# Expert results added into the output tensor, and router products with the weights stationary

## The chip, the cores and the metric

The kernel runs on one core of a Trainium2 chip. The metric is the time of one execution on the device in microseconds (us), as the median of several runs; the profile is of one more execution.

## The reference

A graph layer with 6250 nodes of 256 features (f32) and 100000 edges, followed by a mixture of experts. In short:

```python
xn = layernorm(x)
x = x + gnn(xn, W, edges) + linear_attention(xn, wq, wk, wv, wo)
z = layernorm(x)                       # 6250 x 256
logits = z @ Wr + br                   # 8 experts
top_p, top_idx = top_k(softmax(logits), 2)
weights = top_p / top_p.sum(-1)
zn = layernorm(z)                      # then one gain and bias for each expert
y_e = gelu((zn * g_e + b_e) @ W1_e + b1_e) @ W2_e + b2_e     # 256 -> 1024 -> 256
x = x + sum over the 2 picks of weights * y_pick
```

## The kernel before

The kernel is one program with an instruction stream written out by hand for each engine; semaphores order them. Tokens are cut into 49 tiles of 128 (the last has 106), and each stage streams over tiles. The stages in time:

- To about 490 us: edge lists are sorted, tokens normalized and projected. To about 1555 us: 832 chunks of gathered rows are summed by destination group (line 1437) and added into `acc` in SBUF, with the attention output beside them.
- **Router stage**, 1555 to about 1626 us. DVE computes statistics in four groups of tiles. ACT writes each normalized tile into `xs2` (two tiles make a pair, four pair buffers). For each pair TensorE transposes the four 128x128 blocks (`transpose_x2`, line 1470), ACT copies them from PSUM to `x2T` (`transposed_x2`; all ACT calls are recorded under line 1127), and TensorE multiplies (`router_product`, line 1477): for each token tile the 128x128 block of transposed tokens is the stationary operand and the 8 weight columns stream; the two halves of the features accumulate into 8 columns of bank `B[4]`. SP sends each pair of `xs2` to `token_x` in HBM (line 399) and then issues the load of all second-layer weights, 8 MB, into `W2A` (line 401). ACT scales `acc` afterwards.
- **Slot stage**, to about 1700 us. DVE picks the two best experts of each token, ranks the picks within each expert (with two matmuls), and deals them to 105 tiles of 128 slots, each tile of one expert. The experts of the tiles go by way of HBM (`slot_experts`, lines 406 and 408) to `expert_row`; DVE waits for the first of those transfers before `slot_digits`. 98 matmuls (line 1499) put the token and the pick of each slot into slot order. Slots are in token order within an expert. Unused slots get token 0, a pick whose gate is zero, and a row of their own behind the tokens of `sums` (`dump_row`). `sums` is an HBM tensor that SP sets from `acc` (line 426): the layer's result without the experts.
- **Expert stage**, to about 2467 us: for each slot tile t, POOL gathers the tokens (`gather_x`, line 513) and the gates (line 517); TensorE transposes the tokens (line 1518), multiplies with the first weights (line 1530), and, after ACT's gelu, with the second (line 1539); DVE adds the bias, multiplies with the gate and writes `y_out`, two buffers; POOL scatters it with an add in the DMA into `sums` (`scatter_y`, line 524). Each scatter waits for the one before to land, since two of them may hit one row. TensorE's order is: `inputs(0)`, `first_product(0)`, `inputs(1)`, then steps; step t is `first_product(t + 1)`, `inputs(t + 2)`, `second_product(t)`. DVE's is `inputs(0)`, `inputs(1)`, then steps of `inputs(t + 2)` and `outputs(t)`. SP loads the first weights of each tile, 1 MB (line 418), four buffers.
- **End**: SP waits for the last scatters and copies `sums` to the output, HBM to HBM (line 435).

DVE chains dependent small operations with a semaphore: `ch.add` issues one, `ch.sync` waits for all so far, `ch.link` does both.

Of the kernel before, what the change touches and what calls it, by code (L numbers as in the profile page):

```python
# [15 lines left out]
ALU = mybir.AluOpType  # L16
ACT = mybir.ActivationFunctionType
AX = mybir.AxisListType

P = 128  # L20
N_NODES = 6250
# [107 lines left out]
def gps_layer(nc, x, src, dst, src_rest, dst_rest, gnn_w, wq, bq, wkv, bkv, wo, bo,  # L129
              wr, br, ln_gT, ln_bT, w1, b1, w2, b2, out):  # L130
    ctx = ExitStack()
    with ctx:
# [6 lines left out]
        def dram(name, shape, dt):  # L139
            return nc.dram_tensor(name, shape, dt, kind="Internal").ap()  # L140
# [6 lines left out]

        sums = dram("sums", [(NT + 1) * P, D], F32)
        gates = dram("gates", [(PICKS + 1) * P, 1], F32)
# [17 lines left out]
        def grid(area, at, a, b, dt=F32):  # L167
            return piece(area, at, a * b, dt).rearrange("p (a b) -> p a b", b=b)
# [87 lines left out]
        wr_s, br_s = grid(BIG, 5448, KD, E), piece(BIG, 5464, E)  # L256
        stats2 = grid(BIG, 5150, NT, 6)
        expert_m8 = grid(BIG, 4192, NT, E)
        exp_tot, exp_tiles, exp_base, slot_e, exp_i = (piece(BIG, 4592 + 16 * k, E) for k in range(5))
# [7 lines left out]
        slot_at, slot_tile, pick_col = (piece(BIG, 5100 + 50 * k, PICKS, BF16) for k in range(3))  # L267
        row_1, dump_row, dump_pick = piece(BIG, 5250, 1), piece(BIG, 5251, 1), piece(BIG, 5252, 1)
        zero_row = BIG[0:1, 5260:5260 + ST].bitcast(BF16)
        row_f, tok_f, unused, unused_at, pick_f = (piece(BIG, 1600 + 110 * k, ST) for k in range(5))  # L270
        gates_T = BIG[0:NT, 5376:5376 + TOPK * P]
        slot_token, slot_row, slot_pick = piece(SMALL, 700, ST, I32), piece(SMALL, 0, ST, I32), piece(SMALL, 490, ST, I32)
        slot_eI = piece(BIG, 4690, 1, I32)
# [45 lines left out]
        router_in, norm2_ready = sem("router_in"), sem("norm2_ready")  # L319
        x2T_ps, x2T_ready, logit_ps = sem("x2T_ps"), sem("x2T_ready"), sem("logit_ps")  # L320
        res_ready, pc_rows = sem("res_ready"), sem("pc_rows")
        pick_ready, gap_ready, gap_exp, ranks_ps, places_ready = (
# [8 lines left out]
        y_ps, y_free, y_ready, y_sent = sem("y_ps"), sem("y_free"), sem("y_ready"), [sem("y_sent0"), sem("y_sent1")]  # L331
        o_sent = sem("o_sent")
        block = ctx.enter_context(nc.Block())
# [3 lines left out]
        def _(sp):  # L337
# [87 lines left out]
            sp.wait_ge(res_ready, 1)  # L425
            sp.dma_start(sums.rearrange("(t p) d -> p t d", p=P), acc).then_inc(sums_set, 16)
            with sp.Fori(1, ST // 4) as i:
                for s in range(4):
# [4 lines left out]
            sp.wait_ge(y_sent[1], 16 * (ST // 2))  # L433

            sp.dma_start(out.rearrange("(p a) d -> p (a d)", p=125), sums[0:N_NODES, :].rearrange("(p a) d -> p (a d)", p=125)
                         ).then_inc(o_sent, 16)
            sp.wait_ge(o_sent, 16)


        @block.gpsimd  # L440
        def _(pool):
# [78 lines left out]
            def scatter_y(t):  # L520
                pool.wait_ge(y_ready, t + 1)
                if t >= 1:
                    pool.wait_ge(y_sent[(t - 1) % 2], 16 * ((t + 1) // 2))
                pool.indirect_dma_start(sums, bass.IndirectOffsetOnAxis(ap=slot_row[:, t:t + 1], axis=0),  # L524
                                        y_out[t % 2], None, compute_op=ALU.add).then_inc(y_sent[t % 2], 16)

            pool.wait_ge(slots_ready, 1)
            for t in range(4):
                gather_x(t)
            pool.wait_ge(rows_known, 1)  # L530
            pool.wait_ge(gates_out, 32)
            for t in range(3):
                gather_gate(t)
            gather_x(4)
            pool.wait_ge(sums_set, 16)
            for t in range(ST):
# [8 lines left out]
        def _(dve):  # L545
# [479 lines left out]
            ch.add(ts(row_1, pcol, 1.0, ALU.add))  # L1025
            ch.add(ts(dump_row, pcol, float(NT * P + 1), ALU.add))
            ch.add(ts(dump_pick, pcol, float(PICKS * P + 1), ALU.add))
# [41 lines left out]
            dve.sem_inc(slots_ready, 1)  # L1069
            ch.add(dve.scalar_tensor_tensor(out=tok_f, in0=unused, scalar=dump_row, in1=tok_f, op0=ALU.mult, op1=ALU.add))  # L1070
            ch.add(dve.scalar_tensor_tensor(out=pick_f, in0=unused, scalar=dump_pick, in1=pick_f, op0=ALU.mult, op1=ALU.add))
            ch.sync()
            ch.add(dve.tensor_copy(slot_row, tok_f))
            ch.add(dve.tensor_copy(slot_pick, pick_f))
            ch.sync()
            dve.sem_inc(rows_known, 1)
            dve.wait_ge(gates_T_ps, 1)
# [33 lines left out]
            inputs(0, 0)  # L1111
            inputs(1, 1)
            for t in range(4):
                step(t, t)
# [8 lines left out]
        def _(act):  # L1123
# [118 lines left out]
            def transposed_x2(j):  # L1242

                n = min(2, NT - 2 * j)
                act.wait_ge(x2T_ps, j + 1)
                if j >= 4:
                    act.wait_ge(logit_ps, 2 * (j - 4) + 2)
                cp(x2T[j % 4][:, 0:n * KD, :], B[j % 4][:, 0:n * D].rearrange("p (g n) -> p g n", n=P)).then_inc(x2T_ready, 1)

            def roots(k):  # L1250
# [6 lines left out]
            for k, g in enumerate(LGROUPS):  # L1257
                act.wait_ge(norm2_ready, k + 1)
                for t in g:
                    j = t // 2  # L1260
                    if t % 2 == 0 and j >= 4:
                        act.wait_ge(x2T_ps, j - 3)
                        act.wait_ge(xs_out[j % 4], 16 * (j // 4))
                    cp(xs2[j % 4][:, t % 2, :], acc[:, t, :], ACT.Identity, scale=rstd2[:, t:t + 1], bias=nmr2[:, t:t + 1]
                       ).then_inc(xs_ready, 1)
                    if t % 2 == 1 and t >= 3:
                        transposed_x2(t // 2 - 1)
                    if t == g.stop - 3 and k + 1 < len(LGROUPS):
                        roots(k + 1)
            transposed_x2(NPAIR - 2)  # L1270
            transposed_x2(NPAIR - 1)
            for t in range(NT):
                last = cp(acc[:, t, :], acc[:, t, :], scale=dinv[:, t:t + 1])
# [31 lines left out]
        def _(pe):  # L1305
# [166 lines left out]

            def router_product(j):
                pe.wait_ge(x2T_ready, j + 1)
                for t in range(2 * j, min(2 * j + 2, NT)):
                    for k in range(KD):
                        last = mm(B[4][:, t * E:(t + 1) * E], x2T[j % 4][:, t % 2 * KD + k, :], wr_s[:, k, :],  # L1477
                                  start=k == 0, stop=k == KD - 1)
                    last.then_inc(logit_ps, 1)

            transpose_x2(0)
            for j in range(NPAIR):
                if j + 1 < NPAIR:
                    transpose_x2(j + 1)
                router_product(j)

            pe.wait_ge(pick_ready, 1)
# [65 lines left out]
            first_product(0, 0)  # L1553
            inputs(1, 1)
            step(0, 0)
            with pe.Fori(0, ST // 4 - 1) as i:
# [32 lines left out]
```

## Time and profile before

| | us |
|---|---|
| median of 3 runs | 2496.47 |
| lowest and highest | 2495.27, 2497.32 |
| profiled execution | 2495.66 |
| its span | 2493.8 |
| busy in the span: TensorE matmuls | 2173.1 (87%) |
| busy: POOL, DVE, ACT | 1381.6, 1156.7, 1143.8 |
| mean granted clock of TensorE | 0.93 |

The span runs from the first to the last recorded instruction; 1.9 us of the execution lie around it. The granted clock is a share of 2.4 GHz. The page has a chain of the work that ended last (half of it TensorE), groups of instructions by line with their busy time, mean duration and the idle time before them, and DMA issues with the time to their landing. The timeline gives instructions in order of time, neighbours of one kind merged (x32 is 32 of them), with the idle time in front of them and what ended it in brackets. An f32 product of TensorE shows as two records, a transpose as one.

### The profile page before, as it was taken

How to read it: one execution, taken by the hardware profiler on the slowest of the kernel's cores; microseconds unless marked ns; L12 is line 12 of the kernel's file. 1: busy time of each engine (PE TensorE's matmuls, PEld its weight loads, DVE VectorE, ACT ScalarE, POOL GpSimd, SP SyncE). 2: the span in 40 equal slices, each digit the busy share in tenths (PEclk: the TensorE clock that was granted, in tenths of full speed). 3: DMA queues.
4: the chain of work that ended last, by engine and by line, in shares of the span. 5: the costliest groups of instructions: out<-in, count | busy, mean ns of one | idle time of the engine just before them, and what ended most of it. 6: DMA issues, size and time to landing. Idle time of an engine off the chain costs nothing.

```text
span 2493.8 us, 50478 instructions
## 1 busy us (share of the span) xinstructions
PE 2173.1 (87%) x11949; PEld 1764.4 (71%) x11950; DVE 1156.7 (46%) x2139; ACT 1143.8 (46%) x2788; POOL 1381.6 (55%) x1357
## 2 busy tenths in 40 slices
PE   2996896588889999899899996858999999999995
PEld 1764774376766666666666665827999999999995
DVE  8885652155665665666665665362222222222221
ACT  3664114366666666666666664642223233232331
POOL 3420787277777777777777774003445454454542
PEclk9998667799999999999999999558999999999998
DMA  4002000333333333333333337366666665666664
GB/s 145 1 10 41 3 4 3 121 105 105 104 105 105 105 105 105 105 105 105 105 105 105 105 105 86 102 204 229 176 188 174 184 185 174 188 176 182 185 173 139
DMA packets 136541, 296.30 MB, mean 119 GB/s; under 512 B 28594, under 2 KB 78084, under 8 KB 136231
## 3 DMA queue, kind: packets, MB, share of 16 engines
q0 software_dynamic: 67552, 137.24, 21.7%
q1 hardware_dynamic: 68935, 158.44, 19.7%
q8 instruction: 22, 0.36, 0.1%
q14 instruction: 32, 0.26, 0.0%
HBM read 257.91 MB, written 40.92 MB: 120 GB/s over the span
## 4 chain that ended last, share of the span: by engine, by line
PE 50%; POOL 14%; issue 11%; DVE 10%; DVEq 10%; DMA 3%; SPq 1%; ACT 0%; POOLq 0%; ACTq 0%
PE B L1530 15%; PE B L1539 14%; PE B L1437 13%; POOL BIG L504 8%; POOL edge_rows L493 6%; DVE ACC L549 4%; DVEq L880 3%; DVEq L709 2%; DVEq L872 2%; PE B L1499 1%; PE B L1477 1%; DVE W2A L549 1%; PE B L1410 1%; DVE BIG L549 1%; DMA BIG<-table,W2A 1%
## 5 line engine op out<-in xcount | busy, mean ns | idle before, releaser
L504 POOL DMA_INDIRECT BIG<-table,W2A x832 | 786.6, 945 | 298.3 <-issue 224.2
L549 DVE TENSOR_TENSOR ACC<-ACC,B 128x512 f32 x832 | 572.2, 688 | 402.8 <-PE B L1437 295.8
L1127 ACT ACTIVATE BIG<-B,SMALL 128x128 f32<-128x128 f32 (+1 forms) x889 | 251.1, 387 | 523.9 <-PE B L1530 523.9
L1437 PE MATMUL B<-BIG,W2A 128*128 128x256 f32 x1664 | 411.2, 390 | 76.7 <-DVE ACC L549 49.2
L1437 PE MATMUL B<-BIG 128*128 128x256 f32 x1664 | 407.7, 389 | 45.3 <-DMA BIG<-table,W2A 24.1
L1437 PEld LDWEIGHTS B<-BIG,W2A 128*128 128x128 f32 x1664 | 286.4, 189 | 177.7 <-issue 150.4
L1437 PEld LDWEIGHTS B<-BIG 128*128 128x128 f32 x1664 | 294.6, 190 | 150.2 <-issue 110.6
L1530 PEld LDWEIGHTS B<-BIG,W1A 128*128 128x128 f32 x3360 | 393.7, 193 | 7.9 <-DVE BIG L552 2.6
L1530 PE MATMUL B<-BIG,W1A 128*128 128x128 f32 x3360 | 394.5, 276 | 2.0 <-DVE BIG L552 2.0
L1539 PE MATMUL B<-W2A,BIG 128*128 x1680 | 380.2, 379 | 0.8 <-DVE BIG L549 0.7
L524 POOL DMA_INDIRECT sums<-BIG,SMALL x105 | 170.6, 1625 | 335.9 <-DMA sums<-BIG,SMALL 279.2
L1539 PEld LDWEIGHTS B<-W2A,BIG 128*128 128x128 f32 x1680 | 311.0, 190 | 39.4 <-issue 1.4
L1127 ACT ACTIVATE W2A<-W2A 128x256 f32<-128x256 f32 x416 | 177.3, 496 | 199.2 <-PE B L1437 199.2
L1127 ACT ACTIVATE BIG<-W2A 128x256 f32<-128x256 f32 x416 | 177.4, 497 | 173.1 <-PE B L1437 173.1
L493 POOL DMA_INDIRECT edge_rows<-BIG x128 | 158.1, 1235 | 152.3 <-DVEq L765 111.0
L552 DVE TENSOR_SCALAR BIG<-B,SMALL 128x128 f32<-128x128 f32 x210 | 76.6, 407 | 291.4 <-PE B L1518 291.4
L1127 ACT ACTIVATE BIG<-B 128x256 f32<-128x256 f32 (+1 forms) x172 | 65.7, 411 | 292.4 <-PE B L1329 254.2
L549 DVE TENSOR_TENSOR BIG<-B,W1A 128x256 f32<-128x256 f32 x105 | 44.6, 425 | 272.2 <-PE B L1539 272.2
L513 POOL DMA_INDIRECT BIG<-token_x,SMALL x53 | 50.7, 956 | 177.0 <-DVEq L1069 161.1
L1127 ACT ACTIVATE BIG<-BIG,CONST 128x1024 f32<-128x1024 f32 x104 | 119.6, 1150 | 7.7
L1127 ACT ACTIVATE W2A<-W2A,CONST 128x1024 f32<-128x1024 f32 x104 | 119.4, 1148 | 7.7
L517 POOL DMA_INDIRECT BIG<-gates,SMALL x105 | 102.7, 978 | 32.0 <-issue 32.0
(234 smaller groups left out, 2086.8 us busy)
## 6 DMA issues: line engine op xcount, KB each, us to landing
W1A<-in_w SPq DMA_DIRECT2D x105, 1024.0 KB, 5.1
BIG<-table,W2A POOLq DMA_INDIRECT x832
W2A<-in_w SPq DMA_DIRECT2D x1, 8192.0 KB, 26.3
sums<-ACC SPq DMA_DIRECT2D x1, 6400.0 KB, 23.5
out_dram<-sums SPq DMA_DIRECT2D x1, 6250.0 KB, 21.7
token_x<-BIG SPq DMA_DIRECT2D x24, 256.0 KB, 2.1
W2A<-in_x SPq DMA_DIRECT2D x1, 3584.0 KB, 12.8
table<-ACC SPq DMA_DIRECT2D x2, 1792.0 KB, 10.6
```

The source lines that it names most:

```text
L493: pool.indirect_dma_start(edge_rows, bass.IndirectOffsetOnAxis(ap=row_all[:, r:r + 1], axis=0), keysI[0][:, ROW * r:ROW * (r + 1)], None). ...
L504: pool.indirect_dma_start(G[h][:, u, :], None, table, bass.IndirectOffsetOnAxis(ap=dst_T[:, c:c + 1], axis=0)).then_inc(gath[h][u // 2], 16)
L513: pool.indirect_dma_start(x_in[t % 4], None, token_x, bass.IndirectOffsetOnAxis(ap=slot_token[:, t:t + 1], axis=0)).then_inc(xs_in[t % 4], 16)
L517: pool.indirect_dma_start(slot_gate[:, t:t + 1], None, gates, bass.IndirectOffsetOnAxis(ap=slot_pick[:, t:t + 1], axis=0)).then_inc(gate_i ...
L524: pool.indirect_dma_start(sums, bass.IndirectOffsetOnAxis(ap=slot_row[:, t:t + 1], axis=0), y_out[t % 2], None, compute_op=ALU.add).then_i ...
L549: return dve.tensor_tensor(o, a, b, op)
L552: return dve.tensor_scalar(o, a, s1, s2, op0, op1)
L880: dve.drain()
L1127: return nc.scalar.activation(o, i, fn, **kw)
L1437: last = mm(B[u][:, k * D:(k + 1) * D], OH[h % 2][:, u, k * P:(k + 1) * P], G[h][:, u, :], start=True, stop=True)
L1530: last = mm(B[2 * s + c // 4][:, c % 4 * P:(c % 4 + 1) * P], w1_buf[s4][:, k, c * P:(c + 1) * P], x_inT[s][:, k, :], start=k == 0, stop=k ...
L1539: last = mm(B[7][:, 0:D], hidT[s][:, k, :], W2A[:, bass.ds(e * (KH * D) + k * D, D)], start=k == 0, stop=k == KH - 1)
```

## The change

The experts' results are scattered and added into the output tensor itself. `sums`, the final copy and the wait for it are gone; SP sets the output from `acc` in two transfers (48 full tiles, 106 rows). The output has no rows behind the tokens, so unused slots, which still add zero, must add it to token rows that no used slot of the same tile has. For each expert's last tile the kernel finds them: `offset_of` is each used slot's row less its position, `reached` compares it with every position, eight small matmuls count over the partitions, and the count plus the position is the row (`spare_f`). That is a chain on DVE in two halves with the matmuls between them, placed behind `inputs(1, 1)` on DVE and on TensorE. The picks of the slots have a semaphore of their own, `picks_known`; `rows_known` is signalled behind the new chain, and POOL waits for it ahead of the first scatter.

In the router the 8 weight columns are the stationary operand and 256 tokens stream, so logits come out with experts on 8 partitions, in `B[5]` and `B[6]` by turns; ACT copies them to `logits_T` (`transposed_logits`, one pair behind `transposed_x2`), and TensorE transposes them back to tokens (`token_logits`), one tile in one instruction.

```diff
@@ -255,6 +254,7 @@
+        logits_T = [W1A[0:E, R0 + 8 * NE + D * k:R0 + 8 * NE + D * (k + 1)] for k in range(2)]
...
@@ -423,7 +429,8 @@
             sp.wait_ge(res_ready, 1)
-            sp.dma_start(sums.rearrange("(t p) d -> p t d", p=P), acc).then_inc(sums_set, 16)
+            sp.dma_start(out[0:(NT - 1) * P, :].rearrange("(t p) d -> p t d", p=P), acc[:, 0:NT - 1, :]).then_inc(sums_set, 16)
+            sp.dma_start(out[(NT - 1) * P:N_NODES, :], acc[0:LAST, NT - 1, :]).then_inc(sums_set, 16)
...
@@ -431,10 +438,6 @@
             sp.wait_ge(y_sent[0], 16 * (ST // 2 + 1))
             sp.wait_ge(y_sent[1], 16 * (ST // 2))
-
-            sp.dma_start(out.rearrange("(p a) d -> p (a d)", p=125), sums[0:N_NODES, :].rearrange("(p a) d -> p (a d)", p=125)
-                         ).then_inc(o_sent, 16)
-            sp.wait_ge(o_sent, 16)
@@ -521,18 +524,19 @@
-                pool.indirect_dma_start(sums, bass.IndirectOffsetOnAxis(ap=slot_row[:, t:t + 1], axis=0),
+                pool.indirect_dma_start(out, bass.IndirectOffsetOnAxis(ap=slot_row[:, t:t + 1], axis=0),
                                         y_out[t % 2], None, compute_op=ALU.add).then_inc(y_sent[t % 2], 16)
...
-            pool.wait_ge(rows_known, 1)
+            pool.wait_ge(picks_known, 1)
             pool.wait_ge(gates_out, 32)
             for t in range(3):
                 gather_gate(t)
             gather_x(4)
-            pool.wait_ge(sums_set, 16)
+            pool.wait_ge(rows_known, 1)
+            pool.wait_ge(sums_set, 32)
@@ -1067,13 +1070,10 @@
             dve.sem_inc(slots_ready, 1)
-            ch.add(dve.scalar_tensor_tensor(out=tok_f, in0=unused, scalar=dump_row, in1=tok_f, op0=ALU.mult, op1=ALU.add))
             ch.add(dve.scalar_tensor_tensor(out=pick_f, in0=unused, scalar=dump_pick, in1=pick_f, op0=ALU.mult, op1=ALU.add))
             ch.sync()
-            ch.add(dve.tensor_copy(slot_row, tok_f))
-            ch.add(dve.tensor_copy(slot_pick, pick_f))
-            ch.sync()
-            dve.sem_inc(rows_known, 1)
+            ch.link(dve.tensor_copy(slot_pick, pick_f))
+            dve.sem_inc(picks_known, 1)
@@ -1110,6 +1110,36 @@
             inputs(0, 0)
             inputs(1, 1)
+
+            ch.add(dve.scalar_tensor_tensor(out=offset_f, in0=unused, scalar=float(NT * P), in1=row_f, op0=ALU.mult, op1=ALU.add))
+            ch.add(ts(slots_1, iota[:, 0:ST], 1.0, ALU.add))
+            ch.add(ts(last_end, exp_tiles, 0.0, ALU.is_gt))
+            ch.add(dve.memset(ones_2, 1.0))
+            ch.sync()
+            ch.add(ts(offset_f, offset_f, pcol, ALU.subtract))
+            ch.add(tt(last_end, last_end, exp_i, ALU.mult))
+            ch.sync()
+            for e in range(E):
+                ch.add(dve.scalar_tensor_tensor(out=last_of[:, e, :], in0=slots_1, scalar=last_end[:, e:e + 1], in1=offset_f,
+                                                op0=ALU.is_equal, op1=ALU.mult))
+            ch.sync()
+            ch.link(dve.tensor_reduce(offset_of, last_of, axis=AX.X, op=ALU.add))
+            for e in range(E):
+                ch.add(ts(reached[:, e, :], iota, offset_of[:, e:e + 1], ALU.is_ge))
+            ch.sync()
+            dve.sem_inc(spare_ready, 1)
+            dve.wait_ge(spare_ps, 1)
+            ch.link(dve.tensor_copy(before_of, B[5][:, 0:2 * E:2]))
+            for e in range(E):
+                ch.add(ts(last_of[:, e, :], slots_1, last_end[:, e:e + 1], ALU.is_equal, before_of[:, e:e + 1], ALU.mult))
+            ch.sync()
+            ch.link(dve.tensor_reduce(spare_f, last_of.rearrange("p e t -> p t e"), axis=AX.X, op=ALU.add))
+            ch.link(ts(spare_f, spare_f, pcol, ALU.add))
+            ch.link(tt(spare_f, spare_f, unused, ALU.mult))
+            ch.link(tt(spare_f, spare_f, row_f, ALU.add))
+            ch.link(dve.tensor_copy(slot_row, spare_f))
+            dve.sem_inc(rows_known, 1)
+
             for t in range(4):
                 step(t, t)
@@ -1244,8 +1274,16 @@
                 if j >= 4:
-                    act.wait_ge(logit_ps, 2 * (j - 4) + 2)
+                    act.wait_ge(logitT_ps, j - 3)
                 cp(x2T[j % 4][:, 0:n * KD, :], B[j % 4][:, 0:n * D].rearrange("p (g n) -> p g n", n=P)).then_inc(x2T_ready, 1)
+
+            def transposed_logits(j):
+
+                n = min(2, NT - 2 * j)
+                act.wait_ge(logitT_ps, j + 1)
+                if j >= 2:
+                    act.wait_ge(logit_ps, 2 * (j - 2) + 2)
+                cp(logits_T[j % 2][:, 0:n * P], B[5 + j % 2][0:E, 0:n * P]).then_inc(logitT_ready, 1)
@@ -1265,10 +1303,15 @@
                     if t % 2 == 1 and t >= 3:
                         transposed_x2(t // 2 - 1)
+                        if t >= 5:
+                            transposed_logits(t // 2 - 2)
...
             transposed_x2(NPAIR - 2)
+            transposed_logits(NPAIR - 3)
             transposed_x2(NPAIR - 1)
+            transposed_logits(NPAIR - 2)
+            transposed_logits(NPAIR - 1)
@@ -1471,18 +1514,29 @@
             def router_product(j):
+                n = min(2, NT - 2 * j)
                 pe.wait_ge(x2T_ready, j + 1)
+                if j >= 2:
+                    pe.wait_ge(logitT_ready, j - 1)
+                for k in range(KD):
+                    last = mm(B[5 + j % 2][0:E, 0:n * P], wr_s[:, k, :], x2T[j % 4][:, k:n * KD:KD, :],
+                              start=k == 0, stop=k == KD - 1)
+                last.then_inc(logitT_ps, 1)
+
+            def token_logits(j):
+                pe.wait_ge(logitT_ready, j + 1)
                 for t in range(2 * j, min(2 * j + 2, NT)):
-                    for k in range(KD):
-                        last = mm(B[4][:, t * E:(t + 1) * E], x2T[j % 4][:, t % 2 * KD + k, :], wr_s[:, k, :],
-                                  start=k == 0, stop=k == KD - 1)
-                    last.then_inc(logit_ps, 1)
+                    nc.tensor.transpose(B[4][:, t * E:(t + 1) * E], logits_T[j % 2][:, t % 2 * P:(t % 2 + 1) * P], ident[0:E, 0:E]
+                                        ).then_inc(logit_ps, 1)
...
                 router_product(j)
+                if j > 0:
+                    token_logits(j - 1)
+            token_logits(NPAIR - 1)
@@ -1552,6 +1606,10 @@
             first_product(0, 0)
             inputs(1, 1)
+            pe.wait_ge(spare_ready, 1)
+            for e in range(E):
+                last = mm(B[5][:, 2 * e:2 * e + 2], reached[:, e, :], ones_2, start=True, stop=True)
+            last.then_inc(spare_ps, 1)
             step(0, 0)
```

## Rows read from the trace of the kernel before

**Rows 1.** The page's costliest groups: TensorE in the expert stage.
```profile
L1530 PE MATMUL B<-BIG,W1A 128*128 128x128 f32 x3360 | 394.5, 276 | 2.0 <-DVE BIG L552 2.0
L1539 PE MATMUL B<-W2A,BIG 128*128 x1680 | 380.2, 379 | 0.8 <-DVE BIG L549 0.7
```

**Rows 2.** Timeline (start us, us, what), the end of the span.
```profile
2471.64 0.58 SPq L435 DMA_DIRECT2D out_dram<-sums  x1
```

**Rows 3.** Windows: stretch, its us, busy of each engine, PEclk, DMA, GB/s.
```profile
1548.00:1552.00 4.00, 2.06 (x9) 1.46 (x9) 1.87 (x4) 0.00 (x0) 0.00 (x0) 1.00 0.66 58
...
1556.00:1560.00 4.00, 0.00 (x0) 0.00 (x0) 3.50 (x16) 0.21 (x1) 0.00 (x0) 0.84 0.00 0
...
1608.00:1612.00 4.00, 4.00 (x21) 4.00 (x22) 0.00 (x0) 2.24 (x6) 0.00 (x0) 0.50 0.19 66
...
1644.00:1648.00 4.00, 0.00 (x0) 0.00 (x0) 3.64 (x11) 1.29 (x2) 0.00 (x0) 0.50 0.66 201
...
1704.00:1708.00 4.00, 3.10 (x21) 2.86 (x20) 0.71 (x2) 0.99 (x1) 1.60 (x2) 0.81 1.06 371
```

**Rows 4.** Timeline of the router stage.
```profile
1570.45 1.09 ACT L1127 ACTIVATE BIG<-ACC,SMALL 128x256 f32<-128x256 f32 x2 [3.22 <-DVEq L946]
...
1608.41 1.09 PE L1470 MATMUL B<-CONST,BIG 128*128 128x128 f32 x4
...
1609.30 1.72 PE L1477 MATMUL B<-BIG 128*128 128x8 f32 x8
...
1609.55 0.60 ACT L1127 ACTIVATE BIG<-B 128x512 f32<-128x512 f32 x1 [0.88 <-PE B L1470]
...
1610.04 1.08 ACT L1127 ACTIVATE BIG<-ACC,SMALL 128x256 f32<-128x256 f32 x2
...
1619.85 0.59 ACT L1127 ACTIVATE BIG<-ACC,SMALL 128x256 f32<-128x256 f32 x1
...
1623.84 0.38 ACT L1127 ACTIVATE BIG<-B 128x256 f32<-128x256 f32 x1 [1.43 <-PE B L1470]
...
1626.26 0.57 DVE L549 TENSOR_TENSOR W1A<-B,SMALL 128x392 f32<-128x392 f32 x1 [25.84 <-PE B L1477]
```

**Rows 5.** Timeline where the expert stage begins.
```profile
1700.82 6.06 PE L1530 MATMUL B<-BIG,W1A 128*128 128x128 f32 x32 [1.01 <-DVE BIG L552]
...
1707.29 0.73 DVE L552 TENSOR_SCALAR BIG<-B,SMALL 128x128 f32<-128x128 f32 x2 [6.52 <-PE B L1518]
...
1708.07 3.84 PE L1530 MATMUL B<-BIG,W1A 128*128 128x128 f32 x32 [0.97 <-DVE BIG L552]
...
1721.19 1.64 POOL L524 DMA_INDIRECT sums<-BIG,SMALL  x1 [15.28 <-DMA sums<-ACC]
```

**Rows 6.** Timeline around the transfer of the slot numbers.
```profile
1643.96 0.33 SPq L406 DMA_DIRECT2D slot_experts<-BIG  x1
...
1651.76 0.21 DVE L1036 CAST BIG<-BIG 128x98 bf16<-128x98 int32 x1
...
1652.04 0.25 SPq L408 DMA_DIRECT2D CONST<-slot_experts  x1
```

**Rows 7.** Timeline: DVE and TensorE operations like the added ones.
```profile
1645.90 0.56 DVE L1015 TENSOR_REDUCE SMALL<-W1A 128x49 f32<-128x392 f32 x1
...
1649.98 0.10 PEld L1494 LDWEIGHTS B<-BIG 1*128 1x128 bf16 x1 [12.83 <-DVEq L1030]
...
1694.09 0.46 DVE L552 TENSOR_SCALAR BIG<-BIG 128x105 f32<-128x105 f32 x3
...
1695.52 0.33 DVE L1070 SCALAR_TENSOR_TENSOR BIG<-BIG 128x105 f32<-128x105 f32 x1 [0.16 <-DVE SMALL L1068]
```

**Rows 8.** The tile `sums`: its scatters and what released them.
```profile
L524 POOL DMA_INDIRECT sums<-BIG,SMALL x105: 1570/1627/1650, 1721.2 to 2467.9; - x105
...
  DMA sums<-BIG,SMALL: 279.2, 92
...
DMA to landing us min/median/max: 3.7/6.5/23.5
```

More of the change, by code:

```diff
@@ L146, in gps_layer @@
         token_x = dram("token_x", [NT * P, D], F32)
-        sums = dram("sums", [(NT + 1) * P, D], F32)
         gates = dram("gates", [(PICKS + 1) * P, 1], F32)
@@ L267, in gps_layer @@
         slot_at, slot_tile, pick_col = (piece(BIG, 5100 + 50 * k, PICKS, BF16) for k in range(3))
-        row_1, dump_row, dump_pick = piece(BIG, 5250, 1), piece(BIG, 5251, 1), piece(BIG, 5252, 1)
+        row_1, dump_pick = piece(BIG, 5250, 1), piece(BIG, 5252, 1)
         zero_row = BIG[0:1, 5260:5260 + ST].bitcast(BF16)
@@ L271, in gps_layer @@
         gates_T = BIG[0:NT, 5376:5376 + TOPK * P]
+        last_of, last_end = grid(W1A, R0, E, ST), piece(W1A, R0 + 840, E)
+        spare_f, slots_1, offset_f = (piece(W1A, R0 + 850 + 110 * k, ST) for k in range(3))
+        offset_of, before_of = piece(W1A, R0 + 1180, E), piece(W1A, R0 + 1190, E)
+        reached = grid(W1A, R0 + 1200, E, P, BF16)
+        ones_2 = piece(W1A, R0 + 1720, 2, BF16)
         slot_token, slot_row, slot_pick = piece(SMALL, 700, ST, I32), piece(SMALL, 0, ST, I32), piece(SMALL, 490, ST, I32)
@@ L320, in gps_layer @@
         x2T_ps, x2T_ready, logit_ps = sem("x2T_ps"), sem("x2T_ready"), sem("logit_ps")
+        logitT_ps, logitT_ready = sem("logitT_ps"), sem("logitT_ready")
         res_ready, pc_rows = sem("res_ready"), sem("pc_rows")
@@ L331, in gps_layer @@
         y_ps, y_free, y_ready, y_sent = sem("y_ps"), sem("y_free"), sem("y_ready"), [sem("y_sent0"), sem("y_sent1")]
-        o_sent = sem("o_sent")
+        spare_ready, spare_ps, picks_known = sem("spare_ready"), sem("spare_ps"), sem("picks_known")
         block = ctx.enter_context(nc.Block())
@@ L1025, in _ @@
             ch.add(ts(row_1, pcol, 1.0, ALU.add))
-            ch.add(ts(dump_row, pcol, float(NT * P + 1), ALU.add))
             ch.add(ts(dump_pick, pcol, float(PICKS * P + 1), ALU.add))
```

## The prediction

> **What bounds the kernel now.** I read the page first, for its chain and its costliest groups, then the timeline of the three places that the change touches. In the expert stage TensorE alone sets the pace: its two matmul groups stood idle 2.0 and 0.8 us in 775 us of work [rows 1]. What is saved or lost ahead of that stage, or behind it, moves the end one for one; inside it DVE, ACT and POOL have slack. Behind it stands one transfer: the copy of `sums` to the output is issued at 2471.64 and the span ends at 2493.8, so 22.2 us pass in which no engine computes [rows 2].
>
> The windows [rows 3] give TensorE's granted clock. While it summed chunks with matmuls of 256 moving columns it was at the upper level (1.00) with only 2.06 us of 4 busy. It stopped, and in 1556 to 1560 the clock fell. In the router stage TensorE is busy for 4.00 us of 4, and the clock stays at the lower level, 0.50.
>
> The router stage itself [rows 4]: per pair of token tiles TensorE does 4 transposes in 0.89 us (1608.41 to 1609.30) and 8 records of 128x8 products in 1.72 us, 0.213 us each: every one loads 128 columns of tokens to stream 8. ACT waits for TensorE 0.88 us in each pair. From 1570.45, where DVE releases ACT, to the last normalized tile at 1619.85 there are 21 pairs: 2.35 us each. DVE's pick chain starts at 1626.26, 5.8 us after that last tile (its end, 1620.44).
>
> **The end of the kernel.** The copy goes. The two waits on `y_sent` stay and the new kernel ends there: minus 22.2 us. What loaded `sums` now loads `out`, in two transfers of together as many bytes; I cost that at nothing, because the first scatter at 1721.19 is what waits for it [rows 5], and TensorE doesn't need that scatter for several tiles.
>
> **The router products.** With the 8 weight columns stationary, a pair needs 2 products of 256 moving columns, 4 records (an f32 product is two records). From [rows 1] a 256-column record is 380.2 / 1680 = 0.226 us and a 128-column one 394.5 / 3360 = 0.117 us at the upper clock; at the lower, 0.213 us for 128 columns [rows 4] and so 0.427 for 256. Added are two transposes back to tokens (128 columns loaded, 8 streamed), at most 0.117 or 0.213 us each. TensorE's pair:
> - lower clock: 4 x 0.213 + 4 x 0.427 + 2 x 0.213 = 2.99 us, or 2.8 if one load hides under a product. Slower than now: the exchange by itself saves nothing, 8 x 0.213 against 4 x 0.427.
> - upper clock: 4 x 0.117 + 4 x 0.226 + 2 x 0.117 = 1.61 us.
>
> So the clock decides. The new stage streams 256-column matmuls back to back, which is nearest to the chunk sums, where 1.00 was granted with half of the time busy [rows 3]; and in the expert stage, which began at the lower clock, it rose within a few us (0.81 over 1704 to 1708). I take the upper clock from about the third pair on. The Trainium skill speaks against that, in "TensorE: Matmul & The Clock Gate", Part 1: it explains the clock by how busy the engine has been, so that a busy engine is released to 2.4 GHz. By that rule the present stage, 100% busy, should have had 2.4 GHz; the trace shows 0.50. If what kept this stage down (the rule doesn't say what) also holds for its successor, the case is the cold rival below.
>
> At the upper clock ACT becomes the bound. Its pair is the transposed copy, 0.49 us from start to start (1609.55 to 1610.04), two normalizations, 1.08, and the new copy of 8x256 from PSUM, for which the nearest row is the 128x256 copy of 0.38 [rows 4]. Sum 1.95 us; where neighbours overlap by 0.1 us, as these do, 1.75. I take 1.85, above TensorE's 1.61. Gain: 21 x (2.35 - 1.85) = 10.5 us; with 1.75 it is 12.6, and with 2.1, if the hand-overs between the engines don't hide, 5.3.
>
> **What becomes late next.** With TensorE no longer behind, logits are ready about 3 us after the last tile instead of 5.8. That is not worth another 2.9 us. DVE now reaches its wait for the slot numbers' DMA at 1651.97, and that DMA lands at 1652.04, 8.1 us after its issue at 1643.96 [rows 6]. The 8 MB load of W2 is ahead of it on SP's queue, and the DMA engines still move 201 GB/s on average in 1644 to 1648 [rows 3]. W2 starts with the last tile, not with the logits, so the landing is tied to the last tile (31.6 us behind it), and the saved 2.9 us turn into waiting. Bounds: 0 and minus 2.9; I take 0.
>
> **The spare rows.** Unused slots now need real rows that no used slot of their tile has. DVE computes them after the inputs of tile 1 (their row is 1707.29 with 0.73, so from 1708.02), and TensorE waits for the first half behind `inputs(1, 1)`, ahead of the first product of tile 1, which started at 1708.07 [rows 5]. The first half, from [rows 7]:
> - four small operations at 0.15 each (0.46 for three) and a sync: 0.65; two more with a sync: 0.32
> - 8 scalar_tensor_tensor on 128x105: a lone one is 0.33, independent neighbours run at 0.15 to 0.33; 8 x 0.25 and the tail, 2.1
> - the reduction of 840 elements: 0.56 for 392, of which I take 0.15 as fixed, gives 1.05
> - 8 comparisons on 128x128 at 0.15 and the sync: 1.3
>
> Sum 5.4 us. Then TensorE loads 8 bf16 weights at 0.10 and streams two columns each: 0.9. So product 1 starts 6.3 us later. Bounds: 5 (all overlapped) to 9 (all at full length, and slow loads). TensorE idles over 6 us meanwhile, and after the last such rest the clock had fallen [rows 3]. The first product of tile 0 ran mostly at the lower clock and took 6.06 us against 3.84 for the second [rows 5]: 2.2 us lost. I take the same again, 2.2 (bounds 0 and 4). Together plus 8.5 us on the path.
>
> The second half (a copy, 8 operations of 0.15, a reduction of 1.05, four linked ones of 0.3: 3.8 us) lies beside product 1, and what it holds up on DVE's queue is `inputs(2)`, whose transposes come only after product 1. On POOL `rows_known` now comes at about 1718, before the output's load at 1721: no cost; were that cover gone, scatter 0 would only come later by the difference, and DVE has a second output buffer before it waits for it. The gate gathers wait for `picks_known`, two DVE operations earlier than before; TensorE waited for the token gather there, so nothing.
>
> **Sum.** -22.2 - 10.5 + 8.5 = -24.2 us. The profiled execution took 2495.66 us, 1.9 more than its span, and the median is 2496.47, 0.8 above it; against the profiled time that is 2471.5, against the median 2472.3.
>
> **Rivals.**
> - *Cold router.* The clock stays at 0.50. For it: the stage has stood there for 60 us with TensorE fully busy. Against: the chunk sums and the expert stage. The pair then costs 2.8 to 3.0, 21 x 0.55 = 11.5 us more, and about 1 us more behind it. Total -22.2 + 8.5 + 12.5 = -1.2: 2495, no difference that can be measured.
> - *The scatters become the bound (slower).* Place: POOL's accumulate, now into `out`. 105 of them start from 1721.2 to 2467.9, one in 7.18 us, TensorE's pace, and 92 of them were released by the landing of the one before [rows 8]. If an accumulate into the output tensor lands later than into the internal one, the pace follows it: above 7.2 us per scatter, each extra 0.1 us costs 10.5 us, less about 5 us that the two buffers take up. It decides from 0.32 us extra on; with 0.5 us the whole is -24 + 52 - 5 = +23: 2519. For it: no row shows an accumulate into `out`. Against: as many rows of as many bytes, in the same memory, and median landing is 6.5.
> - *A half-warm case.* The clock rises and falls again within the router stage, or the stall at the entry costs 13 instead of 8.5: each worth about 5 us, so 2477 to 2483. Still faster.
> - *The copy's end is not all saved.* Nothing in the code puts anything in its place, so I give this no chance of its own.
>
> **How the numbers follow.** Forecast 0.75 with 2472.3. Its own ends: -22.2 - 12.6 - 2.9 + 5 = -32.7 (2464), and -22.2 - 5.3 + 13 = -14.5 (2482). Half-warm 0.07, cold 0.12, scatters 0.06. The range 2464 to 2487 takes in the forecast and the half-warm case, and a part of the bad side of their unknown costs; cold and scatters are left out, 0.18. A change of 0.2% (5 us) is about what can be told from none here. Faster by more: 0.75 + 0.07 + a quarter of cold (its lower bounds) = 0.85; same 0.09; slower 0.06.
>
> **What would show it.** Right: SP issues nothing after the last scatter and the span ends within 1 us of its landing; the windows of the router stage show 1.00 from the third or fourth pair on, ACT busy nearly all of it, the pair at 1.85 us; a DVE wait for the slot numbers' landing of 2 to 3 us; TensorE idle for about 6 us in front of the 8 spare-row products, with 0.50 behind it; scatters still one in 7.2 us. Wrong: 0.50 all through the router stage with a pair of 2.9 us; scatters further apart; or a wait for the spare rows much above 6 us.

## The result and the profile after

The changed kernel takes 2475.27 us (median of 6 runs, 2473.08 to 2476.56) against 2495.87 for the kernel before (6 runs, 2494.67 to 2497.32). The ratio is 0.9917, 95% interval 0.9905 to 0.9929: about 20.6 us less. The forecast was 2472.3, in a range from 2464 to 2487.

The page of the changed kernel, the groups that answer to [rows 1] and [rows 8]:

```profile
L1584 PE MATMUL B<-BIG,W1A 128*128 128x128 f32 x3360 | 397.4, 277 | 1.0 <-DVE BIG L556 1.0
L1593 PE MATMUL B<-W2A,BIG 128*128 x1680 | 380.1, 379 | 0.7 <-DVE BIG L553 0.7
L527 POOL DMA_INDIRECT out_dram<-BIG,SMALL x105 | 170.7, 1626 | 343.9 <-DVE BIG L556 343.9
```

TensorE still sets the pace of the expert stage: its two groups stood idle for 1.0 and 0.7 us beside 777 us of work. The scatters, 92 of which had been released by the landing of the one before [rows 8], are now all released by DVE.

Windows of the changed kernel, with the columns of [rows 3]:

```profile
1564.00:1568.00 4.00, 4.00 (x18) 1.82 (x17) 4.00 (x14) 2.73 (x7) 0.00 (x0) 0.69 0.61 199
1568.00:1572.00 4.00, 1.66 (x11) 0.80 (x9) 3.24 (x17) 2.14 (x5) 0.00 (x0) 1.00 0.03 12
1608.00:1612.00 4.00, 2.55 (x16) 1.24 (x15) 1.14 (x3) 2.84 (x9) 0.00 (x0) 1.00 0.91 296
1696.00:1700.00 4.00, 0.00 (x0) 0.00 (x0) 3.93 (x15) 1.46 (x6) 0.00 (x0) 0.53 1.06 367
...
1708.00:1712.00 4.00, 4.00 (x26) 3.64 (x25) 1.20 (x4) 1.70 (x7) 0.00 (x0) 1.00 0.79 283
```

The clock rises within the first pairs, is at 1.00 from 1568 on and stays there to the end of TensorE's router work, 1608 to 1612 included, where it had been 0.50. Behind the new stall at the entry to the expert stage it is low (0.53 over 1696 to 1700), and back at 1.00 over 1708 to 1712.

The timeline of the router stage, one steady pair, to be held against [rows 4]:

```profile
1569.86 1.09 ACT L1157 ACTIVATE BIG<-ACC,SMALL 128x256 f32<-128x256 f32 x2 [2.55 <-DVEq L950]
...
1584.77 0.57 ACT L1157 ACTIVATE BIG<-B 128x512 f32<-128x512 f32 x1
...
1585.25 0.36 ACT L1157 ACTIVATE W1A<-B 8x256 f32<-8x256 f32 x1
1585.51 1.08 ACT L1157 ACTIVATE BIG<-ACC,SMALL 128x256 f32<-128x256 f32 x2
...
1585.67 1.03 PE L1522 MATMUL B<-BIG 128*8 128x256 f32 x4
1586.49 0.57 ACT L1157 ACTIVATE BIG<-B 128x512 f32<-128x512 f32 x1
```

ACT's three kinds of work now follow each other without a gap: the copy of the transposed tokens at 1584.77, the copy of the logits at 1585.25, two normalizations at 1585.51, and the next copy at 1586.49, 1.72 us after the first. TensorE's four records of 256 columns take 1.03 us (1585.67), where the eight of 8 columns took 1.72. Where that stage ends:

```profile
1606.38 0.58 ACT L1157 ACTIVATE BIG<-ACC,SMALL 128x256 f32<-128x256 f32 x1
...
1607.36 0.44 SPq L407 DMA_DIRECT2D W2A<-in_w  x1
...
1610.79 0.57 DVE L553 TENSOR_TENSOR W1A<-B,SMALL 128x392 f32<-128x392 f32 x1 [17.47 <-PE B L1529]
```

Pair 3 begins at 1569.86 and the last tile at 1606.38: 36.52 us for 21 pairs, 1.74 each, where it was 2.35. Logits are complete at 1610.79, 3.8 us behind the end of the last tile. The slot numbers, to be held against [rows 6]:

```profile
1628.49 0.40 SPq L412 DMA_DIRECT2D slot_experts<-BIG  x1
...
1636.23 0.21 DVE L1039 CAST BIG<-BIG 128x98 bf16<-128x98 int32 x1
...
1638.78 1.93 DVE L553 TENSOR_TENSOR BIG<-BIG 128x1792 bf16<-128x1792 bf16 x2 [2.34 <-DMA slot_experts<-BIG]
```

DVE has finished what doesn't need them at 1636.44 and starts the slot digits at 1638.78. Their transfer's landing stands 31.8 us behind the last tile's end (1606.96), and 31.6 before. The entry to the expert stage, against [rows 5]:

```profile
1687.53 6.33 PE L1584 MATMUL B<-BIG,W1A 128*128 128x128 f32 x32 [1.01 <-DVE BIG L556]
...
1694.27 0.73 DVE L556 TENSOR_SCALAR BIG<-B,SMALL 128x128 f32<-128x128 f32 x2 [6.79 <-PE B L1572]
...
1695.82 2.00 DVE L1123 SCALAR_TENSOR_TENSOR W1A<-W1A 128x105 f32<-128x105 f32 x8
...
1698.92 1.66 DVE L556 TENSOR_SCALAR W1A<-CONST,W1A 128x128 bf16<-128x128 f32 x8
...
1700.69 0.37 PE L1611 MATMUL B<-W1A 128*128 128x2 bf16 x8 [6.61 <-DVEq L1130]
...
1700.92 6.45 PE L1584 MATMUL B<-BIG,W1A 128*128 128x128 f32 x32
...
1707.42 3.62 PE L1593 MATMUL B<-W2A,BIG 128*128 x16
```

The spare rows' first half ends with the comparisons at 1700.58, the eight small products start at 1700.69 and are hardly to be seen, and product 1 takes 6.45 us. The end, against [rows 2]:

```profile
2457.79 3.72 PE L1593 MATMUL B<-W2A,BIG 128*128 x16 [0.73 <-DVE BIG L553]
...
2462.96 1.57 POOL L527 DMA_INDIRECT out_dram<-BIG,SMALL  x1 [2.90 <-DVE BIG L556]
```

```profile
SPq L132 <- PEq L132: 5.7, 1, 5.7
SPq L132 <- DMA out_dram<-BIG,SMALL: 4.5, 1, 4.5
```

The second pair are SP's waits: 4.5 us for the last scatters, whose landing SP saw at 2466.8, and 5.7 us in the closing barrier of the program, which the view puts down to TensorE's queue. TensorE's own closing record had ended at 2461.6, though; POOL's records, below, show who came last. The span ends at 2472.7, 9.7 us after the last scatter began; before, the copy was issued 3.7 us after it.

Term by term, from the two profiled executions (spans 2493.8 and 2472.7):

| | forecast | measured |
|---|---|---|
| up to the router's pair 3 (1570.45, 1569.86) | 0 | -0.6 |
| 21 pairs | -10.5 | -12.9 |
| last tile to the slot digits, and on to the first product | 0 | +0.2 |
| entry: first product of tile 0 to second product of tile 0 (11.1 us, 19.9 us) | +8.5 | +8.8 |
| from there to the last scatter | 0 | -0.4 |
| last scatter to the end of the span (25.8 us, 9.7 us) | -22.2 | -16.1 |
| sum | -24.2 | -21.0 |

### The profile page after: what moved, and what is told of

Same layout as the page of the kernel before. It is cut to its first block, busy times and chain, and to the rows that moved or that the text cites. A ratio compares the mean times of both kernels' runs of the same rounds, so it can differ in the third digit from the quotient of the medians.

```text
span 2472.7 us, 50507 instructions
## 1 busy us (share of the span) xinstructions
PE 2159.0 (87%) x11910; PEld 1729.7 (70%) x11911; DVE 1166.6 (47%) x2173; ACT 1148.6 (46%) x2813; POOL 1382.8 (56%) x1357
## 4 chain that ended last, share of the span: by engine, by line
PE 50%; POOL 13%; issue 11%; DVE 10%; DVEq 10%; DMA 3%; SPq 1%; ACT 0%; POOLq 0%; ACTq 0%
PE B L1584 15%; PE B L1593 15%; PE B L1480 13%; POOL BIG L507 7%; POOL edge_rows L496 6%; DVE ACC L553 4%; DVEq L884 3%; DVEq L713 2%; DVEq L876 2%; PE B L1553 2%; DMA BIG<-table,W2A 1%; DVE W2A L553 1%; PE B L1453 1%; DVE BIG L553 1%; PE B L1572 1%
## 5 line engine op out<-in xcount | busy, mean ns | idle before, releaser
L527 POOL DMA_INDIRECT out_dram<-BIG,SMALL x105 | 170.7, 1626 | 343.9 <-DVE BIG L556 343.9
## 6 DMA issues: line engine op xcount, KB each, us to landing
table<-ACC SPq DMA_DIRECT2D x2, 1792.0 KB, 10.2
```

The lines of the kernel that those rows point to most:

```text
L527: pool.indirect_dma_start(out, bass.IndirectOffsetOnAxis(ap=slot_row[:, t:t + 1], axis=0), y_out[t % 2], None, compute_op=ALU.add).then_in ...
```

## The experiments

Ratios are to the kernel before, measured beside them.

**The parts alone.** `router_only` is the kernel before with the router part of the diff only; `output_only` with all the rest of it:

```diff
 (router_only)
-                    last = mm(B[4][:, t * E:(t + 1) * E], x2T[...], wr_s[:, k, :], ...)
+                    last = mm(B[5 + j % 2][0:E, 0:n * P], wr_s[:, k, :], x2T[...], ...)
 (output_only)
-            sp.dma_start(out..., sums...)
+            sp.dma_start(out[0:(NT - 1) * P, :]..., acc[:, 0:NT - 1, :]).then_inc(sums_set, 16)
...
```

Expected of `router_only`:

> Only the router part of the change, on the kernel before. Theory: in the changed kernel the last normalized tile came 13.5 us earlier, 0.6 of it from the stage before, and the later landing of the slot numbers passed on no more than that; so 12.9 us less than the kernel before, about 2483. Rival (the prediction's size of this term): 10.5 us less, about 2485.5. If the two parts of the change help or hurt each other, it differs from 12.9 by more than 1.5 us.

Measured: 2481.30 us against 2494.54, ratio 0.9949 [0.9936, 0.9963]; 13.2 us less. That is nearer to the theory, but the interval, about 9 to 16 us, holds the rival's 10.5 too. The size of 12.9 rests on the trace of the changed kernel. In the profiled execution of `router_only` (2484.34 us, above the median) the 21 pairs took 38.05 us and not 36.52: the clock had risen (0.90 over 1568 to 1572), fell back once and rose for good.

```profile
1572.00:1576.00 4.00, 4.00 (x15) 1.64 (x14) 3.96 (x13) 3.65 (x8) 0.00 (x0) 0.57 0.39 133
```

Expected of `output_only`:

> Only the output part of the change, on the kernel before. Theory: the removed copy had covered the drain that ends POOL's program (9.7 us from the last scatter), so the end gives back 16.1 us and not 22.2; the stall at the entry to the expert stage costs 8.8 us; together 7.3 us less than the kernel before, about 2488.5. Rival (the prediction's sum for this part, 22.2 less 8.5): 13.7 us less, about 2482. The span should end 9 to 10 us behind the last scatter by the theory, 4 to 5 us by the rival.

Measured: 2485.21 us against 2494.54, ratio 0.9962 [0.9949, 0.9976]; 9.3 us less, between the two theories in time and 2 us from the first. The trace decides between them: the last scatter starts at 2474.53 and the span ends at 2484.3, 9.7 us later, as the theory says. (Its first product of tile 0 ran partly at the upper clock and took 5.87 us instead of 6.33; the profiled execution's own time was 2486.2.) The parts add up within their intervals, of about 3 us to either side: 13.2 and 9.3 make 22.5, against 20.6 for both.

**What the end waits for.** Each engine's program closes with an instruction that the trace records as DRAIN. The timeline leaves it out. POOL's, start and duration in us, beside its last scatter:

```
changed kernel   2462.956 1.571 GpSimd DMA_INDIRECT   2462.733 9.744 GpSimd DRAIN
kernel before    2467.936 1.570 GpSimd DMA_INDIRECT   2467.713 9.742 GpSimd DRAIN
pool_waits       2461.453 1.571 GpSimd DMA_INDIRECT   2465.533 7.943 GpSimd DRAIN
```

The drain was there before too, and ended at 2477.5, beneath the copy. ACT and TensorE close with drains of 1.4 and 2.8 us that are over before the last scatter starts; POOL's only other drain, at the start of the program, took 0.17 us. `pool_waits` makes the closing one begin later:

```diff
                 if t + 5 < ST:
                     gather_x(t + 5)
+            pool.wait_ge(y_sent[0], 16 * (ST // 2 + 1))
```

> The changed kernel with one wait more at the end of POOL's program, for the landing of the last scatter, so that POOL's closing drain begins 3.7 to 4 us later; all waits and transfers else are the same. Theory A: the drain takes 9.74 us counted from its own start, whatever is in flight: the end comes 3.7 to 4 us later, about 2479. Theory B: the drain waits for something that the last scatter has set off: it becomes shorter by as much as it begins later, and the time stays at 2475.

Measured: 2475.61 us, ratio 0.9925 [0.9912, 0.9939], which by itself can't be told from the changed kernel's 0.9917. The trace can be read more sharply: from the last scatter to the end of the span it is 12.2 us, against 9.7. The drain isn't shortened by what it no longer covers: it takes 7.94 us from its start, and in the other kernels it ends 7.95 us behind the end of the scatter's instruction (2464.53 to 2472.48), since it is recorded as begun before that instruction. By the time it began in `pool_waits`, at 2465.53, the last scatter had landed, so it isn't the landing that it waits for. Theory B is out and theory A holds; its size was 2.5 and not 4 us, because I had counted from the recorded start. The last scatter itself happened to come 1.5 us earlier in this execution.

Whether an earlier drain takes work off the last one, on the kernel `best` that follows below:

```diff
             gather_x(4)
+            pool.drain()
             pool.wait_ge(rows_known, 1)
             pool.wait_ge(sums_set, 32)
```

> The kernel 'best' with one explicit drain of POOL in its idle time between the first gathers and the first scatter, 16 us long and covered by other work. POOL's closing drain now stands 7.94 us behind its last scatter's own end in every run. Theory A: it costs 7.94 us whatever came before: two drains of about 7.9 us in the trace, time as for best, 2464. Theory B: it settles all indirect DMAs issued since the last drain (1170 of them): the first takes 6 to 7 us, the closing one only a third (2 to 3 us), the time is about 5 us less, 2459.

Measured: 2465.60 us, ratio 0.9874 [0.9859, 0.9889], the same as `best` within the intervals. Two drains stand in the trace, one ending 7.2 us after the last gather, the closing one 7.4 us after the end of the last scatter's instruction. So theory B, with 2 to 3 us for the closing one, is out, and nearly all of the cost comes again with each drain; about 0.5 us was taken off. On the same chip the changed kernel was run again:

> The changed kernel once more, unedited, beside the last variant on one chip, so that the differences of a few us between the runs of different calls can be read: 2475 on both theories, 11 us above best.

Measured: 2476.02 us, ratio 0.9917 [0.9903, 0.9930]: the same ratio as in the first measurement, and 10.4 us above `drain_mid`.

**The entry to the expert stage.** `spare_early` moves one call on DVE:

```diff
             inputs(0, 0)
-            inputs(1, 1)
 
             ch.add(dve.scalar_tensor_tensor(out=offset_f, ...))
...
             dve.sem_inc(spare_ready, 1)
+            inputs(1, 1)
             dve.wait_ge(spare_ps, 1)
```

> The changed kernel with the first half of the spare-row chain on DVE ahead of inputs(1) instead of behind it, beside TensorE's first product of tile 0; TensorE's program is the same. Theory: DVE is idle for 6.8 us there and the half takes 5.7, so TensorE's wait vanishes, the clock stays at 1.00, and all of the 8.8 us at the entry come back: about 2466.5. Rival: the chain delays inputs(1) and the DMA traffic or the clock costs as much whatever the order, so that less than 4 us come back: 2471 or more.

Measured: 2466.81 us, ratio 0.9887 [0.9872, 0.9902], 27.7 us less than before. The chain on DVE stands in the timeline beside the first product of tile 0:

```profile
1689.24 6.14 PE L1584 MATMUL B<-BIG,W1A 128*128 128x128 f32 x32 [1.01 <-DVE BIG L556]
...
1693.11 1.66 DVE L556 TENSOR_SCALAR W1A<-CONST,W1A 128x128 bf16<-128x128 f32 x8
...
1696.30 0.73 DVE L556 TENSOR_SCALAR BIG<-B,SMALL 128x128 f32<-128x128 f32 x2 [1.53 <-PE B L1572]
...
1697.08 3.84 PE L1584 MATMUL B<-BIG,W1A 128*128 128x128 f32 x32 [1.30 <-DVE BIG L556]
```

Product 1 starts 7.84 us after the first product, where it was 7.25 before and 13.4 in the changed kernel, and takes 3.84 us: no stall and no low clock. The theory holds. The chain's comparisons end at 1694.8. About 0.6 us of the cost remains, DVE being a little later with its part of `inputs(1)`.

`keep_busy` leaves the stall and gives TensorE something to do in it:

```diff
             inputs(1, 1)
+            for _ in range(12):
+                mm(B[4][:, 0:2 * P], ident, CONST[:, 0:2 * P], start=True, stop=True)
             pe.wait_ge(spare_ready, 1)
```

> The changed kernel with 12 products of 256 columns from constants into an unused bank, ahead of TensorE's wait for the spare rows (their results are not used). Theory: the wait is as long as before, but the engine isn't at rest, the clock stays at 1.00 behind it, and product 1 takes 3.6 us instead of 6.45: about 2.6 us less than the changed kernel, 2472.7. Rival: the clock's fall costs nothing on the path, and the time is the same or longer, 2475 to 2477.

Measured: 2471.54 us, ratio 0.9910 [0.9895, 0.9925]; 23.0 us less than before, 2.4 more than the changed kernel gains. The intervals of the two overlap, so the time alone shows nothing; the timeline shows the mechanism:

```profile
1692.14 5.34 PE L1610 MATMUL B<-CONST 128*128 128x256 f32 x24
...
1698.92 0.35 PE L1613 MATMUL B<-W1A 128*128 128x2 bf16 x8 [1.43 <-DVEq L1130]
...
1699.13 3.82 PE L1584 MATMUL B<-BIG,W1A 128*128 128x128 f32 x32
```

The small products end the same wait, and product 1 behind them takes 3.82 us instead of 6.45, with the clock at 1.00 over 1696 to 1700, where the changed kernel had 0.53. So the stall of 8.8 us is 6.1 of waiting and 2.6 of clock. (Product 0, ahead of the stall, took 5.39 us here and 5.4 to 6.6 in the eleven traces, with no edit of its own; so by this alone one execution can be 1 us shorter than another.)

**Clock or operands.** In the router two things changed at once: which operand is loaded, and the clock. `old_router_fillers` keeps the old products and adds columns to stream behind each pair:

```diff
                     last.then_inc(logit_ps, 1)
+                for _ in range(2):
+                    mm(B[7][:, 0:2 * P], ident, CONST[:, 2 * P:4 * P], start=True, stop=True)
```

> The kernel before with its own router products (128 columns loaded for 8 streamed), and behind each pair two products of 256 columns from constants into an unused bank (their results are not used): as many streamed columns as the changed router has, on top of the old work. Theory (the gain in the router is the clock's, not the exchange of the operands): the clock rises to 1.00 in this stage, a pair costs 12 x 0.112 + 4 x 0.226 = 2.24 us, and in spite of the added work the kernel is as fast as before or 2 us faster, 2491 to 2495. Rival (the 8-column products hold the clock down whatever streams beside them): 0.50, a pair costs 12 x 0.213 + 4 x 0.427 = 4.27 us, 38 to 40 us more than before, about 2534.

Measured: 2491.28 us (10 runs) against 2494.68, ratio 0.9987 [0.9978, 0.9997]. The kernel before with 100 records of work added to the engine that bounds this stage is no slower, and by 3.4 us in the median faster. The rival, 2534, is out. The windows of the profiled execution (2499.15 us, the slowest of the ten):

```profile
1576.00:1580.00 4.00, 4.00 (x17) 3.53 (x16) 1.65 (x6) 1.31 (x4) 0.00 (x0) 0.50 0.19 66
1584.00:1588.00 4.00, 4.00 (x30) 3.70 (x31) 1.64 (x11) 2.54 (x6) 0.00 (x0) 1.00 0.20 68
```

TensorE is busy for 4.00 us of 4 in both; for the first 20 us of the stage the clock is at 0.50, then it rises, and stays. A steady pair after that is 2.20 us, from the 8-column products of one to those of the next:

```profile
1592.03 0.96 PE L1477 MATMUL B<-BIG 128*128 128x8 f32 x8
...
1592.84 1.11 PE L1481 MATMUL B<-CONST 128*128 128x256 f32 x4
...
1594.23 0.96 PE L1477 MATMUL B<-BIG 128*128 128x8 f32 x8
```

The fillers start 0.81 us after the start of the eight records, which took 1.72 us in the kernel before [rows 4]. Without fillers, 12 records of the old kind at 0.112 us make 1.35 us for a pair, under ACT's pace (an estimate, not run: nothing held the clock up there). By this estimate the gain is the clock's, and the exchange of operands is one way to get it. What in the new stage, or in the fillers, lets the clock rise no run separates.

**A version that beats both.** `best` is `spare_early` with the load of W2 behind the slot numbers on SP's queue:

```diff
-            sp.dma_start(W2A[:, :]..., w2...).then_inc(w2_in, 16)
...
             sp.wait_ge(slot_e_in, 16)
+            sp.dma_start(W2A[:, :]..., w2...).then_inc(w2_in, 16)
```

> The kernel with the spare rows' first half early, and besides the 8 MB load of the second-layer weights issued behind the two small transfers of the slot numbers instead of ahead of them. Theory: the slot numbers no longer queue behind 8 MB, DVE's wait of 2.3 us for them goes, TensorE needs those weights only some 45 us later: 2.3 us less than with the spare rows early alone, about 2464.5. Rival: the load now meets the first loads of the first-layer weights and delays the first tiles' work, or the slot numbers take 10 us anyway: 2467 or more.

Measured: 2464.25 us against 2494.68, ratio 0.9879 [0.9864, 0.9895]. That is 2.6 us less in the median than `spare_early`, 2.0 by the ratios, whose intervals overlap; so the time doesn't show this step's gain, only the timeline does, in which DVE no longer waits:

```profile
1627.73 0.33 SPq L410 DMA_DIRECT2D slot_experts<-BIG  x1
...
1635.08 0.24 SPq L412 DMA_DIRECT2D CONST<-slot_experts  x1
...
1635.71 1.93 DVE L553 TENSOR_TENSOR BIG<-BIG 128x1792 bf16<-128x1792 bf16 x2
...
1638.43 0.39 SPq L414 DMA_DIRECT2D W2A<-in_w  x1
```

The slot numbers land 7.35 us after their issue, with nothing of size in flight, and DVE needs them only at 1635.7. In the changed kernel they took 10.2 us (1628.49 to 1638.71). In the nine traces with the load ahead of them they land 31 to 32 us behind the last tile's end, whenever they are issued; in the two without it, 29.

## Why the prediction was right, and where it wasn't

- *What bounds.* Right: the three places moved the end, all else came to less than 1 us each, and the parts tried alone add up within their intervals.
- *The clock in the router.* Right, in place and sign, and it came sooner than I took it: 0.69 over 1564 to 1568, 1.00 from there on. The cold rival is out. The half-warm one is not: in the profiled executions of `router_only` and `best`, with the same router, the clock rose, fell back (0.57 over 1572 to 1576, 0.60 over 1568 to 1572) and rose again. It cost 1.5 us (38.05 and 38.04 us for the 21 pairs, against 36.52) and not the 5 that were put on it. The Trainium skill's rule ("TensorE: Matmul & The Clock Gate", Part 1: a busy engine is released) fits the changed kernel, busy for 4.00 us of 4 at 1.00 in the steady pairs, but neither the kernel before nor the first 20 us of `old_router_fillers`, where TensorE was busy for 4.00 us of 4 at 0.50.
- *The pair.* The term was undersized: 1.74 us and not 1.85, so 12.9 us and not 10.5. The step that was off is the overhead that I put on ACT's sum. Its lower bound, 1.75, with neighbours overlapping by 0.1 us and no hand-over showing, was the truth.
- *What becomes late next.* Right: logits came 2.0 us sooner behind the last tile, and DVE spent it, with a wait of 2.3 us for the slot numbers. `best` takes that wait away. The landing is tied to the last tile as said. But the load ahead in the queue explains only 3 of the 10 us that the transfer took, and less than 1 of the 8.1 in the kernel before; 7.35 remain without it.
- *The spare rows.* Right in sum, 8.8 for 8.5. DVE's chain took 5.7 us for 5.4 (1694.91 to 1700.58); the eight small products 0.2 us instead of 0.9; the clock 2.6 instead of 2.2. The second half was covered by product 1, as said.
- *The end of the kernel.* This step failed. It read "the two waits on `y_sent` stay and the new kernel ends there: minus 22.2 us". It ends with POOL's closing drain, 7.95 us behind the end of the last scatter's instruction, which the copy had covered: minus 16.1. The sign that was named, a span that ends within 1 us of the last landing, did not come: it ended 5.9 us behind it. The rival "the copy's end is not all saved" is what happened, and it had been given no chance. I had asked of every edit what hides it, but not what the removed transfer itself was hiding. The rows that I read show only engines at work and DMAs; a drain is neither.
- *The scatters.* They did not become the bound, and an accumulate into the output tensor is not slower: its median landing was 3.8 or 6.4 us against 6.5 (last section).

The forecast of 2472.3 was 3.0 us too low, and it came that near because two errors were opposite: 6.1 us at the end and 0.5 at the entry and the slot numbers, less 2.4 of the pairs and 1.0 that the stages around the change happened to take less, make 3.2 between the profiled executions.

## What to carry to other kernels

When the last transfer is taken away, look for what ended beneath it: each engine's closing drain and the barrier. Here it was POOL's, whose last work is an indirect DMA. When a small helper computation is added between engines, put it where the engine that computes it waits for the other anyway; one call moved here was worth about 8 us. And before rewriting slow matmuls, look at the granted clock of their stage: here the old products, at the upper clock, took about half of their time, and even work that was of no use paid for itself by raising it.

## What the runs showed that I had not expected

- POOL's closing drain ended 7.4 to 7.9 us behind the instruction of its last indirect DMA in every kernel, and an additional one in mid-kernel 7.2 us. What it does in that time no run shows, nor whether it would be short behind other work; only the one at the program's start, 0.17 us, had no indirect DMA ahead of it.
- The scatters have two regimes at the same pace. In `output_only` all were released by DVE and landed in 3.8 us; in `spare_early`, into the same tensor, 93 were released by the landing of the one before, which took 6.4, as in the kernel before (6.5, [rows 8]).

```profile
  DVE BIG L554: 343.8, 105
...
DMA to landing us min/median/max: 3.7/3.8/5.0
```

```profile
  DMA out_dram<-BIG,SMALL: 278.6, 93
...
DMA to landing us min/median/max: 3.7/6.4/7.3
```

The second regime was seen where the first scatter had to wait for the load of the output or of `sums`, but `keep_busy` had that wait too and fell into the first. What selects it was not tried. From the second product of tile 0 to the last scatter it is 756.0 us in the second regime (the kernel before) and 755.5 in the first (the changed kernel), so it costs next to nothing here. But a median landing of 6.5 us is close to TensorE's 7.2 us for a tile.

- 128 slot numbers of 4 bytes took 7.35 us to land with no transfer of size in flight (DMA share 0.02 at most over 1628 to 1636 in `best`).
- The clock took about 20 us of the filler variant's router stage to rise (1563.9 to 1584, in the one execution that was profiled), and 3 to 6 us in the eight traces of the new router. Two of these show the fall described above.
